# The second attention's plan: a block's reciprocal deviation as a third piece, and its statistics two steps earlier

## The reference

```
x = x + tanh(g_xattn[0]) * attn0(layernorm(x), ctx, mask)
x = x + tanh(g_ffn[0])   * ffn0(layernorm(x))        # shared expert + 64 routed experts, 8 per row
x = x + tanh(g_xattn[1]) * attn1(layernorm(x), ctx)  # 16 heads of 32, no mask, no output projection
x = x + tanh(g_ffn[1])   * ffn1(layernorm(x))
layernorm(x) = (x - mean) / sqrt(var + 1e-5)
attn1: softmax(Q K^T / sqrt(32)) V, with Q = layernorm(x) wq^T and K, V from ctx
```

## Time and profile before

| | us |
|---|---|
| median of 3 runs | 2937.43 (2934.68 to 2937.49) |
| the profiled execution | 2938.59, its span 2936.9 |
| granted TensorE clock, mean over the span | 0.975 of full speed |
| second attention, scores of unit 0 to unit 63 (starts of the first maximum) | 1696.5 to 2055.3 |
| PE busy over the span | 2718.4 (93%) |
| DVE busy | 1644.6 (56%) |
| ACT busy | 1528.2 (52%) |

### The profile page before, as it was taken

One profiled execution on the slowest core, in us unless ns is written; L12 is line 12 of the kernel. 1 busy time (PEld: TensorE's weight loads), 2 busy tenths in 40 slices (PEclk: granted clock), 3 DMA queues, 4 the chain that ended last, 5 costly groups with the idle time before them and its releaser, 6 DMA issues. The chain is left out here.

```text
span 2936.9 us, 47196 instructions
## 1 busy us (share of the span) xinstructions
PE 2718.4 (93%) x18014; PEld 1539.6 (52%) x18014; DVE 1644.6 (56%) x2727; ACT 1528.2 (52%) x3658; POOL 1038.5 (35%) x824
## 2 busy tenths in 40 slices
PE   6989987999999989999999878888899999999999
PEld 4544543444444457777777555555344444444444
DVE  7888875755555356665555468787463233342332
ACT  5888884323333146666666379888343223332231
POOL 2444451365545646666666301011102011220111
PEclk8999998999999999999999889999999999999999
DMA  4021004111111269999999701100410000000000
GB/s 151 20 67 34 34 16 153 62 46 47 47 48 34 75 204 283 287 287 289 285 283 293 175 1 44 45 30 29 159 61 1 29 29 1 29 29 29 15 1 29
DMA packets 152272, 277.74 MB, mean 95 GB/s; under 512 B 19953, under 2 KB 28913, under 8 KB 152049
## 3 DMA queue, kind: packets, MB, share of 16 engines
q1 hardware_dynamic: 115184, 207.39, 20.1%
q0 software_dynamic: 36864, 67.34, 10.9%
HBM read 198.86 MB, written 75.89 MB: 94 GB/s over the span
## 5 line engine op out<-in xcount | busy, mean ns | idle before, releaser
L1345 POOL DMA_INDIRECT ids<-sh_tk,sh_su x256 | 270.3, 1056 | 279.9 <-PE sh_gu L53 88.8
L53 PE MATMUL ex_gu<-ex_xT,ex_h 128*128 128x256 f16 x3072 | 345.8, 273 | 2.9 <-issue 1.9
L53 PE MATMUL sh_gu<-sh_zT,sh_wgu 128*128 128x512 f16 x1536 | 340.7, 381 | 1.3 <-DVE sh_wgu L1251 0.7
L53 PEld LDWEIGHTS ex_gu<-ex_xT,ex_h 128*128 128x128 f16 x3072 | 300.3, 98 | 51.6 <-issue 3.1
L1684 POOL DMA_INDIRECT xp<-ex_oo,ex_to x128 | 239.9, 1874 | 177.6 <-ACT ex_oo L1625 131.9
L2243 POOL TENSOR_TENSOR fe_prodT<-fe_pp,fe_prodT 128x512 f16<-128x512 f32 x64 | 75.7, 1183 | 605.5 <-ACT fe_prodT L2007 605.5
L496 PE MATMUL at_g<-id,at_p 128*128 128x128 f32 x1280 | 211.2, 292 | 61.7 <-POOL at_p L865 23.9
L53 PEld LDWEIGHTS sh_gu<-sh_zT,sh_wgu 128*128 128x128 f16 x1536 | 149.8, 98 | 178.3 <-issue 4.1
L496 PEld LDWEIGHTS at_g<-id,at_p 128*128 128x128 f32 x1280 | 166.8, 170 | 133.7 <-issue 40.7
L1479 DVE SCALAR_TENSOR_TENSOR ex_h<-ring,ex_h 128x1024 f16<-128x1024 f32 x128 | 151.1, 1222 | 150.3 <-ACT ex_h L1469 150.3
L654 ACT ACTIVATE at_s<-at_s,at_mx 128x154 f32<-128x154 f32 x512 | 210.5, 417 | 0.1
(11 more groups left out here) (277 smaller groups left out, 5165.8 us busy)
## 6 DMA issues: line engine op xcount, KB each, us to landing
ring<-L_ffn_expert_gate_up_w SPq DMA_DIRECT2D x64, 1024.0 KB
ring<-L_ffn_expert_down_w SPq DMA_DIRECT2D x64, 512.0 KB
ring<-x SPq DMA_DIRECT2D x24, 1024.0 KB, 5.6
x<-ring SPq DMA_DIRECT2D x16, 1024.0 KB, 5.2
zrows<-sh_zs SPq DMA_DIRECT2D x32, 256.0 KB
xp<-ring SPq DMA_DIRECT2D x8, 1024.0 KB
ring<-xp SPq DMA_DIRECT2D x8, 1024.0 KB, 6.3
out<-ring SPq DMA_DIRECT2D x8, 1024.0 KB, 4.2
```

The source lines that it names most:

```text
L53: mm = nc.tensor.matmul(out, lhs(a, k), rhs(b, k), start=start and i == 0 and j == 0, stop=stop and i == n - 1 and j == 2)
L1345: e.indirect_dma_start(ids, bass.IndirectOffsetOnAxis(slotu[b % 2][:, t, j:j + 1], 0), pair[b % 2][:, t, j, :], None, bounds_check=SLOTS - ...
```

## The change

In the second attention alone, `stats` gets a third part. Part 0 and part 1 are as before but for the reciprocal, which is now part 2, one step later. For blocks 3 to 7 all of it starts two steps earlier: parts in steps 8(b-2)-2, -1 and 0 where they were in 8(b-2) and +1. Block 2 keeps its steps 1 and 2 and has the reciprocal in step 3. Blocks 0 and 1 have the three parts one right behind the other in the same place as before. The first attention keeps its two parts.

```diff
             if b == 0:
-                at(-1, "stats", 0, 0)
-                at(-1, "stats", 0, 1)
+                for i in range(2 if L0 else 3):
+                    at(-1, "stats", 0, i)
...
             if b:
-                for i in range(2):
-                    at(max(n + turns[0] - early - 2 + i, 0), "stats", b, i)
+                for i in range(2 if L0 else 3):
+                    at(max(n + turns[0] - early - (2 if L0 or b < 3 else 4) + i, 0), "stats", b, i)
...
                 if what == "stats":
-                    if k:
+                    if k == 1:
                         nrm.scalar_deviation(B)
...
                 if what == "stats":
-                    nrm.vector_stats(B, k)
-                    if k:
+                    if k < 2:
+                        nrm.vector_stats(B, k)
+                    if k == (1 if L0 else 2):
                         nrm.vector_rstd(B)
```

## The result

| | before | after |
|---|---|---|
| median on the same chip | 2937.62 us (7 runs) | 2923.07 us (7 runs) |
| ratio, 95% interval | | 0.9951, 0.994 to 0.9962 |
| profiled execution's span | 2936.9 us | 2919.8 us |
| VectorE's wait for the root, blocks 3 to 7 | 6.8 us in 5 | none |
| TensorE's wait for exponentials (L580), units 9 to 63 | 16.1 us in 10 | 5.5 us in 9 |

The change makes the kernel faster by 14.4 us (11.2 to 17.6 us); 7.4 us were forecast.

The account below looks back on a forecast made before the run. PE is busy 93% of the span, but ScalarE alone was taken to hold the second attention's steps around the square root. Five blocks' 7.2 us plus 0.2 us gave 7.4 us, so 2930.0 us; range 2927.5 to 2935.5.

Parts of the forecast that it names:

- What the statistics cost: Second attention: a block's statistics cost 3.14 us, 15.7 us in five blocks, the most any placing could bring.
- Part 0 in step 30: Two bn_stats between VectorE's copies in step 30 cost 0, or 1.2 us if all cover were gone.
- The square root in step 31: Root and loads moved to step 31 start unit 32's exponentials 1.83 us late; ScalarE's 1.06 us idle covers the rest.
- 1.45 us a block: Unit 34's exponentials start at 1903.18 instead of 1904.63; blocks 3 to 7 together gain 7.2 us.
- Which part of the statistics costs what: Three costs: bn_stats delaying step 32's maximum 0.68 us, VectorE's stop for the root, and ScalarE's loads and root in step 33.
- Blocks 1 and 2: Block 2's later reciprocal shifts PSUM banks, removing step 4's zT wait: 0.2 us taken, up to 0.9 us through TensorE.
- End of the stage: Stores, next stage's loads and its first work move along whole with the last blocks; no other transfer sets the end.
- the cover: Rival: step 31's ScalarE idle may not absorb the added work; gain only 1.5 us in all, 2935.9 us; chance 0.22.
- The clock takes it back: Rival: TensorE's moved wait slows the projections of steps 32 and 33; 1.9 us worse per block, 2946.6 us; chance 0.06.
- The clock gives more: Rival: clock drops after TensorE's long waits may go; 9.3 us gain in all, 2928.1 us; chance 0.12.
- The range: Whole kernel: 2927.5 to 2935.5 us, taking in most of one rival and the greater part of another.
- The 1.2 us between the profiled execution and the median: Whole kernel: median 2937.43 lies 1.2 us below the profiled 2938.6, so the predicted 2931.2 became 2930.0 us.

Follow-up runs that it names:

- ahead_one: Kernel after with blocks 3 to 7's statistics one step ahead instead of two; ratio 0.999 (0.9981 to 1.0) to before, period 45.3 us without a clock drop.
- split_only: Kernel before with the reciprocal as a third part one step later, nothing moved ahead; ratio 0.9996 (0.9985 to 1.0006).
- before_notable: Kernel before with Identity for the square root of blocks 3 to 7, so without their table loads; ratio 0.996 (0.9946 to 0.9975), period 44.6 us.
- again_after: The kernel after measured and profiled once more, no edit; ratio 0.9964 (0.9952 to 0.9976) to before.
- keep_b2: Kernel after with block 2 as in the kernel before, reciprocal in step 2; ratio 0.9965 (0.9951 to 0.9979) to before.
- banks_only: Kernel before with an empty piece in step 3, so its turns come later and PSUM banks fall otherwise; ratio 0.999 (0.998 to 1.0).
- newton2: Kernel after with VectorE computing blocks 3 to 7's inverse root by three Newton steps, no ScalarE root or loads; 2911.74 us, ratio 0.9952 to before.

## Why the prediction was wrong in its size, step by step

- *What the statistics cost, 3.14 us a block*: right in the sum. Without loads and two steps ahead a period takes 42.9 us, 3.2 us under before's 46.1.
- *Part 0 in step 30 at no cost*: right. The steps from unit 30 to 32 take 6.2 us each before and after.
- *The square root in step 31, 1.83 us late, with ScalarE's 1.06 us as cover*: right, 1.86 us. ahead_one, with 0.43 us of cover, gains 0.8 us as reckoned.
- *1.45 us a block, 7.2 us in five*: right. Without a drop of the clock the period is 1.5 us shorter, and the stretch from unit 9 to 49 gives 7.6 us, of which some 0.3 us is the clock's (see the rivals).
- *Which part of the statistics costs what*: VectorE's share of step 33 was missing in my account. It named VectorE's stop for the square root as a part of the cost; split_only shows that it cost at most 0.3 us in five blocks. before_notable shows that VectorE's statistics hold step 33 for 1.0 us (5.67 against 4.65) even when the loads are gone. The sum was not touched, because it followed the chain.
- *Blocks 1 and 2, 0.2 us with 0.9 us as the other bound*: **this is the step that failed**; it measured 2.3 to 3.0 us from unit 0 to 5, of which 0.3 to 1.0 us is given back by unit 9. The mechanism was named, the bank that waits for zT, but I took only the 0.23 us that reached ScalarE's copy, and gave TensorE's earlier start as the most. TensorE comes last in this step. From the first maximum of unit 2 to step 4's transposes it is 1723.42 - 1710.27 = 13.15 us before and 1724.26 - 1712.01 = 12.25 us in again_after. The 0.9 us counted in full, and the projection itself was no fixed 4.42 us: begun earlier and with less idle ahead, it took 3.15 us in again_after and 2.75 us in after. 0.9 + 1.3 = 2.2 us. In the step 4 of before the clock was at half speed for most of the projection (0.62), in again_after for a small part (0.87), in after not at all (1.00). Both levels' rows lay side by side, and the bound should have been set with them, 0.9 + 1.67 = 2.6 us; the first profile of the kernel after, with 3.0 us, goes beyond even that, because the transposes ahead of the projection ran faster there too (1.56 us for the eight, 1.95 us in before). The term as measured, from unit 0 to 9, is 61.0 and 61.1 us before and 59.0 to 59.1 us after: 2.0 us for the 0.2 in the sum.

  In the timeline of the kernel before, behind that projection, this could have been read: ScalarE and VectorE both wait for TensorE.

```profile
1729.62 0.60 ACT L625 ACTIVATE at_qT<-at_g 128x512 f32<-128x512 f32 x1 [1.24 <-PE at_g L53]
...
1729.85 0.42 DVE L829 COPY at_pT<-at_g 128x256 f32<-128x256 f32 x1 [2.23 <-PE at_g L496]
```

- *End of the stage moves along whole*: right for the instructions. Its time scatters by 3 us between profiles, and the average of both pairs differs by about 1 us; with the clock dropping in other places I cannot tell gain from chance there.
- *The rivals*: the cover was not gone. *The clock takes it back* came true once in each of the four profiles of the kernel after: of the ten projections in the two steps behind the moved roots one took 4.43 or 4.44 us, behind 0.71 us of idle. The argument against this rival, that no drop follows gaps of about 1 us, held in the trace of before and not in these. It cost little. The period grew by 1.6 us and the next one gave back 0.8; from unit 9 to 49 it is 222.8 us against 222.1 in keep_b2, whose plan is the same from block 3 on and which has no drop there. Why it strikes one block and not the others is not shown. *The clock gives more* was right in part: the four drops of before between unit 9 and 49, behind the 2.16 us waits, are gone. By estimate they cost 1.0 us together (230.4 us, against four periods of 46.1 and a last one of 45.0 us without a drop, as in banks_only). Less the 0.7 us of the new one, some 0.3 us is left.
- *The range*: the terms that can be told from chance, 7.6 and 2.0 us, give 9.6 us and 2927.8 us, just inside the range; with the 1 us at the end of the stage it is 10.5 us and 2926.9 us, 0.6 us below it. So blocks 1 and 2 account for 1.8 us of the miss, and not for its whole. The other 4 to 5 us of the first comparison, 14.4 us, belong to no term: the other three comparisons average 10.9 us, and the stages ahead, which are the same program, differed by 6.3 us in the first pair of profiles. With their differences the time would be 2926.8, 2924.5 and 2928.3 us: below the forecast each time, once inside the range and twice under it by 0.7 and 3.0 us. So what lies between 9.6 and 14.4 us cannot be told from scatter, and its cause stays open. The 1.2 us between the profiled execution and the median played no part.

The Trainium skill, page "ScalarE: Activation LUTs", section "What ACT_TABLE_LOAD costs", states a drain behind each load of a new set. By rows of the kernel after, the square root starts 1.30 us after its load (1876.87 to 1878.17), and the exponential 1.30 us after the other (1879.87 to 1881.17). In these rows no drain is seen, as the prediction had it. The rule of the same page of the Trainium skill, section "Table sets: the hidden batching unit", to group calls by set points the right way all the same: the two loads are the 1.66 us a block that newton2 mostly gets.

## What to carry to other kernels

A piece that must run is cheapest in the step where each engine that it occupies has idle time just ahead of its next due hand-over; read that from the brackets of one period, and follow the chain from there with the distances that the trace has. A wait that an experiment removes without gain (VectorE's for the root) was a sign of where time was lost and not its cause. When an edit changes the order in which a rotating set of buffers is taken, look for the engine that waits for each buffer at the new place, and where that engine is TensorE, price the work behind the wait at both levels of the clock. A gap moved on TensorE can move a drop with it, even when it is short.

## What the hardware showed that I had not expected

- The same projection, 12 matmuls of 128x512, took 2.75, 3.08, 3.15, 4.28, 4.42 and 4.45 us (keep_b2) in step 4, by when the clock came back to 2.4 GHz. A wait of TensorE of 1.1 to 1.7 us in front of that step's transposes goes with the three slow ones. In the steps behind the moved roots 0.71 us of idle was followed once in each profile by 4.43 or 4.44 us, else by 2.75 us.
- The time of stages that the change does not touch moved by up to 9 us from one profiled execution to another, drops of the clock being one part of it. A gain of 10 us in 2930 needs the stretch itself to be measured; medians of 5 to 10 runs of the kernel after left an interval 6 to 10 us wide.
- Twelve dependent VectorE instructions on 128x4, each with a semaphore behind it, ran 0.20 us apart.
